# The right half of x turned in blocks by VectorE, and unit loads issued by GpSimd, in a two-layer conditional residual kernel

## What is computed

```python
# layer 0: one weight W for all, and a mask of 0/1 per batch, scaled by coeff[b]
sign = 2 * mask[b] - 1
h = x + x @ W.T + bias + coeff[b] * (x @ sign)
# layer 1: the adapter that the batch asks for
out = h + h @ weight[ids[b]].T
```

## Time and profile before

| | us |
|---|---|
| median of 3 runs | 403.95 |
| the three runs | 403.78, 403.95, 405.43 |
| the profiled execution, its own time | 405.76 |
| its span (first to last instruction) | 404.0 |

### The profile page before, as it was taken

How to read it: one execution, slowest core, us unless ns; L and a number is a source line. 1 busy time by engine, 2 the same in 40 slices (tenths; PEclk the granted TensorE clock), 3 DMA queues, 4 the chain that set the end, 5 groups by cost and what they waited for, 6 DMA issues and landing times.

```text
span 404.0 us, 7261 instructions
## 1 busy us (share of the span) xinstructions
PE 394.2 (98%) x2578; PEld 360.4 (89%) x2578; DVE 349.5 (87%) x344; ACT 256.1 (63%) x321; POOL 51.1 (13%) x78
## 2 busy tenths in 40 slices
PE   7898999999999999999999999999999999999996
PEld 7898999887899999999999999999999999999885
DVE  0599899979999899989998999988999899988830
ACT  2799876746666676676675577756665785654621
POOL 1112010111111012201010200010010200110100
PEclk9999999999999999999999999999999999999999
DMA  8999867997999999998489947999489984744511
GB/s 224 373 310 315 303 145 181 208 221 228 248 207 284 233 227 243 285 245 244 154 290 256 246 124 215 284 237 233 158 254 261 225 221 151 215 132 138 150 52 52
DMA packets 64630, 88.57 MB, mean 219 GB/s; under 512 B 7250, under 2 KB 48210, under 8 KB 64594
## 3 DMA queue, kind: packets, MB, share of 16 engines
q1 hardware_dynamic: 58752, 79.71, 77.0%
q10 hardware_dynamic: 5842, 8.40, 6.3%
HBM read 79.70 MB, written 8.39 MB: 218 GB/s over the span
## 4 chain that ended last, share of the span: by engine, by line
PE 77%; DVE 11%; ACT 4%; DMA 4%; issue 1%; SPq 1%; POOL 0%; DVEq 0%; POOLq 0%; ACTq 0%
PE second_ps L400 38%; PE first_ps L369 36%; PE turn_ps L352 3%; DVE natural L671 2%; DMA natural<-in_L_cond_weight_dram 2%; ACT masks L473 2%; DVE w_lo_left L675 2%; DMA masks<-in_mask_Bx4096x_ik_dram 2%; DVE masks L656 2%; ACT WT L468 1%; DVE M_lo L664 1%; DVE h_lo L664 1%; DVE x_lo L680 1%; DVE h_lo L687 1%; DVE w_lo_right L664 1%
## 5 line engine op out<-in xcount | busy, mean ns | idle before, releaser
L369 PE MATMUL first_ps<-x_lo,M_hi 128*128 128x256 f32 x416 | 118.4, 285 | 0.6 <-DVE M_lo L664 0.6
L369 PE MATMUL first_ps<-x_hi,M_lo 128*128 128x256 f32 x416 | 117.7, 283 | 0.0
L369 PE MATMUL first_ps<-x_hi,M_hi 128*128 128x256 f32 x416 | 117.7, 283 | 0.0
L488 ACT CAST M_hi<-masks 128x1024 fp32r<-128x1024 f32 (+1 forms) x57 | 57.6, 1011 | 79.9 <-PE first_ps L369 39.6
L656 DVE SCALAR_TENSOR_TENSOR masks<-masks,coeffs,WT 128x1024 f32<-128x1024 f32 x60 | 78.3, 1311 | 13.8 <-ACT WT L468 13.8
L369 PEld LDWEIGHTS first_ps<-x_lo,M_hi 128*128 128x128 f32 x416 | 79.7, 192 | 1.9 <-DVE M_lo L664 0.8
L671 DVE STREAM_TRANSPOSE natural<-natural 128x1024 f32<-128x1024 f32 x64 | 78.9, 1235 | 2.9 <-POOL natural L302 2.9
L302 POOL TENSOR_TENSOR natural<-natural,ident 32x128 f32<-32x128 f32 x64 | 43.7, 683 | 297.4 <-DMA natural<-in_L_cond_weight_dram 297.4
L369 PEld LDWEIGHTS first_ps<-x_hi,M_hi 128*128 128x128 f32 x416 | 79.7, 192 | 0.9
L369 PEld LDWEIGHTS first_ps<-x_hi,M_lo 128*128 128x128 f32 x416 | 79.7, 192 | 0.0
L664 DVE TENSOR_TENSOR M_lo<-masks,M_hi 128x1024 fp32r<-128x1024 f32 (+1 forms) x57 | 66.5, 1167 | 12.7 <-ACT M_hi L488 12.4
(11 more groups left out here) (77 smaller groups left out, 544.3 us busy)
## 6 DMA issues: line engine op xcount, KB each, us to landing
natural<-in_L_cond_weight_dram SPq DMA_DIRECT2D x256, 128.0 KB, 5.0
masks<-in_mask_Bx4096x_ik_dram SPq DMA_DIRECT2D x60, 512.0 KB, 8.2
out_dram<-out_sb ACTq DMA_DIRECT2D x32, 256.0 KB, 4.4
x_nat<-in_x_dram SPq DMA_DIRECT2D x14, 512.0 KB, 7.2
W_nat<-in_L_cond_W_dram SPq DMA_DIRECT2D x8, 512.0 KB, 7.9
natural<-in_mask_Bx4096x_ik_dram SPq DMA_DIRECT2D x4, 512.0 KB, 8.0
natural<-in_x_dram SPq DMA_DIRECT2D x2, 512.0 KB, 9.5
bias_col<-in_L_cond_b_dram ACTq DMA_DIRECT2D x4, 1.0 KB, 6.9
```

The source lines that it names most:

```text
L369: done = nc.tensor.matmul(acc(b, u), left, right, start=(k == 0 and u % 2 == 0 and j == 0), stop=(k == K - 1 and u % 2 == 1 and j == 2))
L488: done = nc.scalar.copy(part.rearrange("p u (a j) -> p a u j", j=SQ), whole[:, :, u0:u0 + part.shape[1], :])
```

## The change

From batch 3 on, the right half of x is no longer turned by TensorE. SP loads it in pieces of 32 numbers (128 bytes) to the places from which one turn in 32x32 blocks by VectorE, in place, makes the whole transpose; ScalarE and VectorE then round it and make its rest from SBUF in place of PSUM. The 16 DMAs for it are issued in the steps i = 3 to 6 of the batch before, four each; the turn is at i = 1 of its own batch, the rounding and the rest at i = 2. The left half stays as it was. And units 14 to 63, which the loop loads, are issued by GpSimd in its own loop, unit g + 3 behind the diagonal of unit g, with semaphores of their own (`natural_pooled`). `x_nat` is laid out half by half; the sizes are the same.

```diff
+POOL_UNIT = 14
+BLOCK_X = 3
...
-        x_nat = sb("x_nat", [P, ST, D], F32)
+        x_nat = sb("x_nat", [P, 2, ST, HALF], F32)
...
+        def wait_unit(engine, g):
+            if g < POOL_UNIT:
+                engine.wait_ge(natural_loaded[g % RING], DMA * GRP * (g // RING + 1))
+            else:
+                engine.wait_ge(natural_pooled[g % RING], DMA * GRP * ((g - POOL_UNIT) // RING + 1))
...
+        x_blocks = x_nat[:, 1, :, :].rearrange("p s c -> p (s c)")
...
+            def load_x_blocks(b, k):
+                if b == BLOCK_X:
+                    sp.wait_ge(x_turned, turned_count(b - 1, 1) + 1)
+                else:
+                    sp.wait_ge(x_done, half_count(b - 1, 1) + 1)
+                for q in range(GRP):
+                    at = HALF + k * P + q * SQ
+                    sp.dma_start(x_blocks[q * SQ:(q + 1) * SQ, k * S:(k + 1) * S].rearrange("r (g j) -> r g j", j=SQ),
+                                 x[b, :, at:at + SQ].rearrange("(g r) j -> r g j", r=SQ)).then_inc(x_loaded[1], DMA)
...
                 if n + RING < CHUNKS:
                     load_mask(n + RING)
-                if n - 2 < CHUNKS:
-                    load_unit(n - 2)
+                if 3 <= i < 7 and b + 1 < B:
+                    load_x_blocks(b + 1, i - 3)
                 if i == 2 and b + 1 < B:
-                    for half in range(2):
-                        load_x(b + 1, half)
+                    load_x(b + 1, 0)
...
+            def load_unit(g):
+                pool.wait_ge(w_done, g - RING + 1)
+                who = pool.value_load(ids_row[0:1, g // K:g // K + 1], min_val=0, max_val=weight.shape[0] - 1)
+                for a in range(GRP):
+                    nc.gpsimd.dma_start(*quadrant(who, g, a)).then_inc(natural_pooled[g % RING], DMA)
...
                 add_diagonal(g)
+                if POOL_UNIT <= g + 3 < CHUNKS:
+                    load_unit(g + 3)
...
                 if i == 4 and b + 1 < B:
                     turn_x(b + 1, 0)
-                if i == 7 and b + 1 < B:
-                    turn_x(b + 1, 1)
...
             def round_x(b, half):
-                act.wait_ge(x_turned, half_count(b, half) + 1)
-                nc.scalar.copy(x_half(x_hi, h_hi, b, half), turned_x).then_inc(x_hi_done, 1)
+                source = turned_x
+                if b >= BLOCK_X and half:
+                    act.wait_ge(first_done, K * b)
+                    act.wait_ge(x_blocks_turned, b - BLOCK_X + 1)
+                    source = x_blocks.rearrange("p (k s) -> p k s", s=S)
+                else:
+                    act.wait_ge(x_turned, turned_count(b, half) + 1)
+                nc.scalar.copy(x_half(x_hi, h_hi, b, half), source).then_inc(x_hi_done, 1)
...
                 round_w(n - 5)
+                if b >= BLOCK_X and i == 2:
+                    round_x(b, 1)
...
+            def turn_x_blocks(b):
+                dve.wait_ge(x_loaded[1], DMA * (2 + K // 2 * GRP * (b - BLOCK_X + 1)))
+                nc.vector.transpose(x_blocks, x_blocks).then_inc(x_blocks_turned, 1)
...
                 rest_w(g)
+                if b >= BLOCK_X and i == 1:
+                    turn_x_blocks(b)
+                if b >= BLOCK_X and i == 2:
+                    rest_x(b, 1)
...
                     rest_h(b)
-                    if b + 1 < B:
-                        rest_x(b + 1, 1)
```

More of the change, by code:

```diff
@@ L90, in build @@
         natural_loaded = [sem(f"natural_loaded{i}") for i in range(RING)]
+        natural_pooled = [sem(f"natural_pooled{i}") for i in range(RING)]
         mask_loaded = [sem(f"mask_loaded{i}") for i in range(OPEN_RING)]
@@ L159, in w_part, with quadrant, x_arrives @@
                     .rearrange("p u (c r) -> p u c r", r=SQ))
[L161 to L166, removed]
+        def wait_unit(engine, g):
[3 more added lines that the diff above has]
+                engine.wait_ge(natural_pooled[g % RING], DMA * GRP * ((g - POOL_UNIT) // RING + 1))
+        def quadrant(who, g, a):
+            m = g % K
+            return (natural[a * SQ:(a + 1) * SQ, g % RING, :].rearrange("r (c f) -> r c f", f=Q),
+                    weight[bass.ds(who, 1), m * P:(m + 1) * P, a * Q:(a + 1) * Q]
+                    .rearrange("a (c r) f -> r (a c) f", r=SQ))
+        def x_arrives(b, half):
+            return natural[:, :ST, half * HALF:(half + 1) * HALF] if b == 1 else x_nat[:, half, :, :]
+        x_blocks = x_nat[:, 1, :, :].rearrange("p s c -> p (s c)")
         def x_part(tile, h, b):
@@ L176, in half_count, with turned_count @@
             return 2 * half + b if b < 2 else 2 * b + half
+        def turned_count(b, half):
+            return half_count(b, half) if b < BLOCK_X else 2 * BLOCK_X + b - BLOCK_X
         turned_x = turn_ps[:, :, :].rearrange("p n (k s) -> p (n k) s", s=S)
@@ L224, in load_unit @@
                 who = sp.value_load(ids_row[0:1, g // K:g // K + 1], min_val=0, max_val=weight.shape[0] - 1)
-                m = g % K
                 for a in range(GRP):
-                    sp.dma_start(natural[a * SQ:(a + 1) * SQ, g % RING, :].rearrange("r (c f) -> r c f", f=Q),
-                                 weight[bass.ds(who, 1), m * P:(m + 1) * P, a * Q:(a + 1) * Q]
-                                 .rearrange("a (c r) f -> r (a c) f", r=SQ)).then_inc(natural_loaded[g % RING], DMA)
+                    sp.dma_start(*quadrant(who, g, a)).then_inc(natural_loaded[g % RING], DMA)
+            def load_x_blocks(b, k):
[7 more added lines that the diff above has]
+                                 x[b, :, at:at + SQ].rearrange("(g r) j -> r g j", r=SQ)).then_inc(x_loaded[1], DMA)
             load_x(0, 0)
@@ L341, in turn_x @@
                 n = half_count(b, half)
-                if b < 2:
+                if b > BLOCK_X:
+                    pe.wait_ge(x_done, half_count(b - 1, 0) + 1)
+                elif b < 2:
                     pe.wait_ge(WT_done, W_BEFORE_X[n])
@@ L350, in turn_x @@
                     for s in range(ST):
[L351 removed]
                         done = nc.tensor.transpose(turned_x[:, k, s * P:(s + 1) * P],
[L353 removed]
+                                                   x_arrives(b, half)[:, s, k * P:(k + 1) * P], ident[:, :])
                 done.then_inc(x_turned, 1)
```

12 lines of the change are left out of this document (6 added, 6 removed).

## The result

The changed kernel takes **401.95 us** (median of 21 runs, 401.38 to 405.52), the kernel before 404.45 beside it on the same chips. The ratio of the two is 0.9942, with a 95% interval of 0.9925 to 0.9960: 0.6% faster, 2.4 us. One of the 21 runs of the kernel before took 484.85 us and is left out of the ratio. The forecast was 399.6, 4.4 us faster. So the direction held and the range did too, but the time lies outside the range that went with the forecast alone (398.8 to 401.5), and the gain is about half of what was forecast.

The account below looks back on a forecast made before the run. TensorE, never idle in a batch, was taken as the bound; five turns left out save 4.4 us, all else hidden, so the median of 403.95 becomes 399.6 us, range 398.7 to 406.0.

Parts of the forecast that it names:

- the forecast alone: The case that the forecast itself comes true, without the rivals: 398.8 to 401.5 us, chance 0.60.
- the price of a turn: TensorE, end of batches 2 to 6: each turn left out saves 0.87 to 0.89 us, five save 4.4.
- The tail: End of the loop: loads of units 62 and 63 delay `rest_w(63)` by 1.7 us, hidden under 2.3 of slack before `second(7, 2)`.
- GpSimd's pace: Units 14 to 63: 0.6 us an issue, 4.5 a unit, hidden in 5.7; break-even at 0.92 an issue.
- VectorE's room: Each batch: 3.3 us idle, less 1.2 for the transpose and 0.9 for the shorter batch, leaves 1.2; added work costs nothing.
- The DMA engines: Loads of x in 128-byte pieces: 39 ns a packet, 9 us more a batch, no loss, only later landings.
- Freeing SP: SP's queue: 27 us a batch taken away, 8.2 us of block issues added; its new wait costs nothing.
- The rivals: Four: GpSimd sets the pace (0.16), VectorE sets the pace (0.12), late transfers (0.07), TensorE's gain handed back at handovers (0.05).
- the second: Rival, VectorE sets the pace: GpSimd's issues lengthen its instructions beyond its room, 403.6 to 405.6 us, chance 0.12.

Follow-up runs that it names:

- the blocks alone: The changed kernel, but SP issues all units as in the kernel before: 399.47 us, ratio 0.9882 to the kernel before; run again, 399.32 us, ratio 0.9863.
- the slower run with three transposes: The blocks alone, but VectorE turns each right half of x three times in place: 410.81 us, ratio 1.0149 to the kernel before.

## Why the prediction was half right

- **What bounds it, and the price of a turn**: right. 0.87 to 0.89 forecast; a batch gets 0.90 shorter by a turn left out and 0.87 longer by one made twice. The loop gives 4.2 us in five, 0.84 each, because batch 6 hands 0.3 back, and 4.5 to 4.8 with the blocks alone. Reading the chain's stretch and not the sum of the instructions' means (2.2 us) was what made it so.
- **The tail**: here the forecast failed. The step named `second(7, 2)` as the place and units 62 and 63 as the cause, and put 1.7 us of delay under 2.3 of slack. With the diagonal of 59 first, that chain behaves as forecast: its end is 1.2 us later and hidden. But the stall came earlier, at unit 59, through an instruction that I had counted as a cost on GpSimd and not as something queued behind a wait. GpSimd works in order: the loads of unit 61 wait for the remainder of unit 57, and the diagonal of 59, ready long before, waits with them. The budget from `rest_w(g-2)` to `turn_w(g)`, 5.9 us, is that of a steady step with one turn. The loop's last step turns two units in succession, and there it is gone. The rows of before quoted above, the transposes' `x2` and the 1.65 us that `rest_h(7)` waited, were there to be read. The term was put at 0 and measured 2.0; exchanging the two instructions gave all but 0.1 of it back.
- **GpSimd's pace**: right. Assumed 0.6 us an issue; measured 0.55, and 0.61 from start to start. The id's read takes 0.95 us and not 1.6, the diagonal 0.86 and not 0.46; the sum, 4.2 us against 4.5, is hidden in 5.7. The Trainium skill's page "SBUF — State Buffer", section "A bandwidth-pool intuition that's wrong (but worth ruling out)", has a DMA issued by GpSimd take about 3100 ns in place of 620 beside a copy by VectorE; the prediction took these as times of an issue. Here, with VectorE busy 98% of a batch, the longest of 200 issues took 692 ns, and the 44 that lie wholly within one 32x32 transpose took 556 at most. The section "Who interferes with whom" of the Trainium skill's page "SBUF — State Buffer" says that an instruction of VectorE with two inputs in SBUF contends with a GpSimd instruction that reads SBUF, and that such instructions were not seen to stall a DMA. The trace agrees with both: the issues keep their 550 ns, and the diagonal, which reads SBUF, is lengthened and lengthens. The prediction used only the half that spares the issues.
- **VectorE's room**: kept, but thinner than said. I took 1.2 us (0.6 if ScalarE's wait stays; it stayed). Beside it came the 0.13 us that a diagonal adds to a unit's remainder, and this is the 0.3 us of batch 6. I had written off this effect because the means of 1.22 stood beside GpSimd's work too. They did not: in the batch of the earlier trace rows none of the eight unit remainders and none of the eight of M ran beside a diagonal. In batches 3 to 6 together 8 of 32 unit remainders did in the kernel before, and 23 of 32 in the changed kernel. What changed is the diagonals' place, not their number.
- **The DMA engines**: cost nothing that showed, as said, though my figure was high. In the blocks-only version SP's queue carries the same bytes in 79152 packets where the earlier trace rows has 58752:

```profile
q1 hardware_dynamic: 79152, 79.72, 82.9%
```

  82.9% of 397.8 us less 77.0% of 404.0 is 18.7 us more in each of 16 engines, for 20400 packets more: 15 ns a packet and not 39. Take that as the difference between these two executions and not as a packet's price: the same 79152 packets took 74.2% of 408.6 us, 303 us, in the slower run with three transposes. In the changed kernel the blocks land in 5.7 us (median) and the masks in 7.1, and no wait for them reached TensorE.
- **Freeing SP**: I credited it with nothing, and the blocks alone show that it was worth nothing.

The rivals: none of the four came true as priced. Of the second, VectorE delayed by GpSimd's work, 0.3 us appeared in one batch, through the diagonals and not the issues. The loss itself had a fifth form, an order and not a rate.

## What to carry to other kernels

When an issue with a wait in it moves to an engine that also computes, list what stands behind that wait in the engine's order, and walk through the irregular steps, the first and the last of the loop above all; a steady-state budget says nothing of them. Take a gain on the bounding engine from the chain's stretches, then ask which half of a combined change brings it: here one half was the whole gain and the other only took from it. An engine at 98% beside one at 100% is not yet a cost, but it has little room for the next idea. And before a mean is called undisturbed by another engine's work, look whether the two ever ran side by side in the stretch that it is from.

## What the runs showed that was not expected

- The diagonal add of GpSimd slows VectorE's two-input remainder from 1226 to 1350 ns, and is itself slowed from 445 to as much as 1537, while DMA issues of the same GpSimd neither suffer (550 to 692 ns) nor, by the run without diagonals, do harm.
- GpSimd pauses once between two issues of one unit. Its timeline in the changed kernel:

```profile
261.65 0.55 POOL L340 DMA_DIRECT2D natural<-in_L_cond_weight_dram  x1 [2.34 <-issue]
264.80 1.78 POOL L340 DMA_DIRECT2D natural<-in_L_cond_weight_dram  x3 [2.60 <-issue]
```

  2.6 us pass with nothing in the profile that would hold it; VectorE's turn then waited 0.85 us. It is no accident of this execution: in every version in which GpSimd issues the units there is one such pause of 2.6 us, beginning 159.5 to 162.8 us behind the loop's first matmul. Its cause was not tried.
- The opening, the same code in all versions, lasted 97.8 to 101.8 us in one execution or another. That is as large as what was measured here, and why a single profile's span could not be used. What varies in it was not settled.
